# Two-part fused kernel: the last output products, the order of work in the first and last pair, and the change of parts are rearranged

## The reference, cut to what matters

```python
lat = layer_norm(_layernorm(x), g_lat, b_lat);  ctx = layer_norm(context, g_ctx, b_ctx)
q = lat @ Wq                       # 16 heads of 64
k, v = split(ctx @ Wkv);  k = apply_rope(k, cos, sin)
attn = softmax(clip(q @ k.T / 8, -11, 11))
x = x + (attn @ v) @ Wo + bo
h = _layernorm(x)
sel = sigmoid(h @ expert_sel.T)                 # (4, 512, 16)
scores = relu(einsum('bsd,edh->bseh', h, keys)) # 16 experts, 256 -> 128
out = x + einsum('bseh,ehv,bse->bsv', scores, values, sel)   # 128 -> 256
```

## Time and profile before

| | |
|---|---|
| runs | 1011.68, 1012.51, 1013.43 us |
| profiled execution, its own time | 1013.12 us |
| its span, first to last instruction | 1011.3 us |
| PE busy | 978.9 us, 97% |
| DVE busy | 809.5 us, 80% |
| ACT busy | 531.8 us, 53% |
| POOL busy | 146.1 us, 14% |
| mean granted clock of PE | 0.996 |
| attention, then experts | change of parts at 817 us |

### The profile page before, as it was taken

One profiled execution on the slowest core, in us unless ns is written; L12 is line 12 of the kernel. 1 busy time (PEld: TensorE's weight loads), 2 busy tenths in 40 slices (PEclk: granted clock), 3 DMA queues, 4 the chain that ended last, 5 costly groups with the idle time before them and its releaser, 6 DMA issues. The chain is left out here.

```text
span 1011.3 us, 16015 instructions
## 1 busy us (share of the span) xinstructions
PE 978.9 (97%) x5712; PEld 620.5 (61%) x5712; DVE 809.5 (80%) x1277; ACT 531.8 (53%) x765; POOL 146.1 (14%) x130
## 2 busy tenths in 40 slices
PE   4999999999999999999999999999999899999998
PEld 3744555555555555555555555555555368889898
DVE  7788999999999989898988887998889876545332
ACT  3666666566665666565656555555555532222221
POOL 3200000000000000000000000320000144444443
PEclk8999999999999999999999999999999999999999
DMA  7343323333232323333333223232222471342331
GB/s 217 111 132 95 111 85 110 103 102 88 77 90 74 89 74 97 89 99 79 97 83 90 64 85 84 84 84 84 85 63 65 131 266 54 126 126 84 115 113 44
DMA packets 68569, 99.84 MB, mean 99 GB/s; under 512 B 21840, under 2 KB 44624, under 8 KB 66448
## 3 DMA queue, kind: packets, MB, share of 16 engines
q1 hardware_dynamic: 68496, 98.89, 32.5%
HBM read 70.01 MB, written 10.75 MB: 80 GB/s over the span
## 5 line engine op out<-in xcount | busy, mean ns | idle before, releaser
L1099 ACT ACTIVATE wide_a<-score_ps 128x1024 f32<-128x1024 f32 x256 | 248.8, 1026 | 118.2 <-PE score_ps L859 118.0
L1401 DVE TENSOR_SCALAR wide_a<-wide_a 128x1024 f32<-128x1024 f32 x256 | 170.3, 691 | 48.1 <-ACT wide_a L1099 47.8
L1410 DVE TENSOR_TENSOR p_sum<-wide_a 128x1024 f32<-128x1024 f32 x128 | 158.5, 1238 | 2.4
L872 PE MATMUL o_ps<-wide_a,v_sb 128*64 128x512 f32 x512 | 124.0, 605 | 0.7 <-issue 0.6
L872 PE MATMUL o_ps<-wide_a,values_a 128*64 128x512 f32 x512 | 124.0, 605 | 0.2 <-issue 0.2
L859 PE MATMUL score_ps<-q_hi,k_hi 64*128 64x512 f32 x512 | 115.0, 445 | 3.3 <-ACT wide_a L1099 1.8
L859 PEld LDWEIGHTS score_ps<-q_hi,k_hi 64*128 64x128 f32 x512 | 47.9, 183 | 114.0 <-issue 79.5
L1917 DVE SCALAR_TENSOR_TENSOR act<-h_ps,wide_a 128x512 f32<-128x512 f32 x64 | 44.1, 690 | 89.2 <-PE h_ps L150 83.8
L1843 ACT CAST act_hi<-act 128x512 fp32r<-128x512 f32 x64 | 39.8, 622 | 138.1 <-DVE act L1917 138.1
L859 PE MATMUL score_ps<-q_hi,k_lo 64*128 64x512 f32 x512 | 101.1, 391 | 0.0
L859 PE MATMUL score_ps<-q_lo,k_hi 64*128 64x512 f32 x512 | 100.4, 388 | 0.0
(11 more groups left out here) (218 smaller groups left out, 1924.6 us busy)
## 6 DMA issues: line engine op xcount, KB each, us to landing
wide_a<-sel_dram SPq DMA_DIRECT2D x16, 1024.0 KB, 4.8
k_swap<-k SPq DMA_DIRECT2D x124, 128.0 KB, 2.3
w_hi<-packs_hi SPq DMA_DIRECT2D x26, 384.0 KB, 3.1
w_lo<-packs_lo SPq DMA_DIRECT2D x26, 384.0 KB, 3.7
den<-inv_dram SPq DMA_DIRECT2D x64, 128.0 KB, 2.9
ctx_raw<-ctx SPq DMA_DIRECT2D x24, 128.0 KB, 2.3
packs_hi<-w_hi SPq DMA_DIRECT2D x8, 384.0 KB, 2.9
packs_lo<-w_lo SPq DMA_DIRECT2D x8, 384.0 KB, 3.4
```

The source lines that it names most:

```text
L872: mm = pe.matmul(o_ps[DH * h:DH * h + DH, :], v_sb[n // 2 % 2][:, at:at + DH], probs[s % RING][:, h, :], start=(s == 0), stop=(s == STEPS ...
L1099: act.activation(probs[s % RING][:], score_ps[s % 2][:], ACT.Exp, scale=DH ** -0.5).then_inc(exp_done, 1)
L1401: dve.tensor_scalar(probs[s % RING][:], probs[s % RING][:], CLIP_HI, CLIP_LO, ALU.min, ALU.max).then_inc(clipped, 1)
L1410: dve.tensor_tensor(p_sum[m][:], first, second, ALU.add).then_inc(summed_up, 1)
```

## The change

In words, following the diff:

- `project_last_y` makes the last two output products (pairs 30 and 31) as one accumulation of six terms per half, at expert 14 of chunk 0. The product of pair 30, which was two products of three matmuls at the end of the attention part with two additions behind them, goes from there; so do two of the four last additions. The second buffers o_hi and o_lo are now shared by both parts.
- The first two expert products of chunk 0 are made at the end of the attention part, into job_ps[0] and job_ps[1]; `gate_h` reads them there. Turning y and x_n into these banks then waits for the gates. The fourth lot of keys has a semaphore of its own, waited on at expert 8.
- In pairs 24 to 27 `head_rows` (only the addition; the statistics are in `head_rows_stats`, at the old place) and `head_split_x` stand before the clips of step 3.
- In the first pair, `split_q(1)` stands after `sum_up` of step 1 and not ahead of `rope_times`, `split_v_weights(1)` after `stats`.
- In pairs 29 to 31, `split_o` stands before `add_y` and the sums of step 0. In the last pair the half product of pair 28 goes to job_ps[1] and that of pair 29 to job_ps[0]; the waits for y_added are loosened accordingly; `scale_o` stands after the second clip of step 3, the addition and `split_keys(3)` after the last sum; ACT rounds o and keys one step later; SP issues two loads of values after `turn_den` of pair 30 instead of before, and reorders the last loads.
- The last chunk's rows are stored in four transfers.

```diff
     product(pe, bank[:], [(hi, o_hi), (hi, o_lo), (lo, o_hi)]).then_inc(sh.y_projected, 1)
+def project_last_y(pe, sh, mt, bank, w_hi, w_lo):
+    wait(pe, sh.o_split, NPAIR)
+    terms = []
+    for n, at in ((NPAIR - 2, WO_AT), (NPAIR - 1, 0)):
+        hi, lo = w_hi[:, at + mt * P:at + mt * P + P], w_lo[:, at + mt * P:at + mt * P + P]
+        o_hi, o_lo = sh.o_hi[n % 2][:], sh.o_lo[n % 2][:]
+        terms += [(hi, o_hi), (hi, o_lo), (lo, o_hi)]
+    product(pe, bank[:], terms).then_inc(sh.y_projected, 1)
+def expert_terms(sh, e, x_hi, x_lo):
+    at = slice(e % 8 * HID, (e % 8 + 1) * HID)
+    terms = []
+    for k in range(KT):
+        hi, lo = sh.wide_hi[:, k, e // 8, at], sh.wide_lo[:, k, e // 8, at]
+        terms += [(hi, x_hi(k)), (hi, x_lo(k)), (lo, x_hi(k))]
+    return terms
...
                     turn_den(sp, sh, n - 1)
+                if n == NPAIR - 1:
+                    sp.wait_ge(pv_done, STEPS * (n - 1))
+                    for lot in (1, 2):
+                        sp.dma_start(sh.values_a[:, (lot - 1) * 4 * D:lot * 4 * D].rearrange("p (e d) -> p e d", d=D),
+                                     values[4 * lot:4 * lot + 4, :, :].rearrange("e h d -> h e d")
+                                     ).then_inc(sh.first_values[lot], DMA)
                 if n > 0:
...
                     load_keys(3)
-                    sp.wait_ge(pv_done, STEPS * n)
-                    for lot in (1, 2):
-                        sp.dma_start(sh.values_a[:, (lot - 1) * 4 * D:lot * 4 * D].rearrange("p (e d) -> p e d", d=D),
-                                     values[4 * lot:4 * lot + 4, :, :].rearrange("e h d -> h e d")
-                                     ).then_inc(sh.first_values[lot], DMA)
...
                 iteration(n)
-            sp.wait_ge(w_fetched, 2 * DMA * (NPAIR + 2 - PAIRS))
-            for dram, t in zip(packs, (sh.w_hi1, sh.w_lo1)):
-                sp.dma_start(raw(t)[:, 0:D], dram[(NPAIR - 1 + WO_LAG) % PAIRS, :, WO_AT:WC]).then_inc(sh.last_wo, DMA)
-            sp.wait_ge(k_split, NPAIR + 1)
-            sp.dma_start(k32[:].rearrange("p (e d) -> p e d", d=D),
-                         values[12:16, :, :].rearrange("e h d -> h e d")).then_inc(sh.first_values[3], DMA)
             sp.wait_ge(sh.gate_stored, DMA)
-            for q in range(2):
+            def first_gates(q):
                 sp.wait_ge(pv_done, STEPS * NPAIR - 2 + 2 * q)
...
                              ).then_inc(sh.first_gates[q], DMA)
+            first_gates(0)
+            sp.wait_ge(w_fetched, 2 * DMA * (NPAIR + 2 - PAIRS))
+            for dram, t in zip(packs, (sh.w_hi1, sh.w_lo1)):
+                sp.dma_start(raw(t)[:, 0:D], dram[(NPAIR - 1 + WO_LAG) % PAIRS, :, WO_AT:WC]).then_inc(sh.last_wo, DMA)
+            first_gates(1)
+            sp.wait_ge(k_split, NPAIR + 1)
+            sp.dma_start(k32[:].rearrange("p (e d) -> p e d", d=D),
+                         values[12:16, :, :].rearrange("e h d -> h e d")).then_inc(sh.first_values[3], DMA)
...
                 wait(pe, den_evac, n)
-                wait(pe, y_added, 2 * (n - 1))
+                wait(pe, y_added, 2 * (n - 1) - (1 if n >= NPAIR - 2 else 0))
                 if n == NPAIR - 1:
...
                 pe.wait_ge(den_evac, n)
-                pe.wait_ge(y_added, 2 * (n - 1))
+                pe.wait_ge(y_added, 2 * (n - 2) + 1)
                 ones_round([(0, p_sum[0]), (1, p_sum[1])], True, False)
...
                         pe.wait_ge(y_added, 2 * (n - 3) + 1)
-                        project_y(pe, sh, n - 3, 1, side_ps, w_hi[n % 2], w_lo[n % 2], (n - 1) % 2)
+                        project_y(pe, sh, n - 3, 1, job_ps[1] if n == NPAIR - 1 else side_ps, w_hi[n % 2], w_lo[n % 2],
+                                  (n - 1) % 2)
                     if m == 0 and p < NPAIR:
...
                     if m == 3 and n == NPAIR - 1:
-                        pe.wait_ge(y_added, 2 * (n - 2) + 1)
-                        project_y(pe, sh, n - 2, 1, side_ps, w_hi[p % 2], w_lo[p % 2], n % 2)
+                        pe.wait_ge(q_split, NPAIR)
+                        project_y(pe, sh, n - 2, 1, job_ps[0], w_hi[p % 2], w_lo[p % 2], n % 2)
                     if m > 0:
...
             pack_ready(NPAIR - 2 + WO_LAG)
-            for mt in range(2):
-                project_y(pe, sh, NPAIR - 2, mt, job_ps[mt], w_hi[1], w_lo[1], 0)
+            pe.wait_ge(sh.key_split, 3)
+            pe.wait_ge(head_split, 2)
+            pe.wait_ge(y_added, 2 * (NPAIR - 2))
+            for e in range(2):
+                product(pe, job_ps[e][:], expert_terms(sh, e, lambda k: xT_hi[:, 0, k, :], lambda k: xT_lo[:, 0, k, :])
+                        ).then_inc(sh.h_ready, 1)
...
                             round_keys((n - 24) // 2)
-                    if n == NPAIR - 1 and m in (1, 2):
-                        round_keys(m + 1)
+                    if n == NPAIR - 1 and m == 3:
+                        round_o(act, act.copy, sh, n - 1, 0)
+                    if n == NPAIR - 1 and m in (2, 3):
+                        round_keys(m)
...
                 iteration(n)
-            round_o(act, act.copy, sh, NPAIR - 2, 0)
             evac_o(NPAIR - 1)
...
                                   ALU.add).then_inc(head_added, 1)
+            def head_rows_stats(t):
...
                         normalize(t, ctx_n[:], x_n[:])
-                    if last and m == 3:
-                        add_y(dve, sh, n - 2, 1, side_ps, bo)
-                        split_keys(3)
+                    if m == 3 and n in (24, 25):
+                        head_rows(2 * (n - 24))
+                    if m == 3 and n in (26, 27):
+                        head_split_x(2 * (n - 26))
                     clip(n, 2 * m)
+                    if n == 0 and m == 0:
+                        rope_first_cos(1)
+                    if m == 1 and p < NPAIR:
+                        rope_times(p)
+                    clip(n, 2 * m + 1)
                     if last and m == 3:
...
                     if n == 0 and m == 0:
-                        rope_first_cos(1)
-                    if m == 1 and n == 0:
-                        split_q(p)
-                    if m == 1 and p < NPAIR:
-                        rope_times(p)
-                    clip(n, 2 * m + 1)
-                    if n == 0 and m == 0:
                         rope_first_sin(1)
+                    if m == 0 and n >= NPAIR - 3:
+                        split_o(dve, sh, n - 2, n % 2)
                     if m == 0 and n >= 3:
-                        add_y(dve, sh, n - 3, 1, side_ps, bo)
+                        add_y(dve, sh, n - 3, 1, job_ps[1] if last else side_ps, bo)
                     if m == 0 and n > 0 and n - 1 not in THREE_PARTS:
...
                         split_k_first(1)
-                        split_v_weights(1)
                     if m == 0:
...
                             stats(t)
-                        if n >= 2:
+                        if n == 0:
+                            split_v_weights(1)
+                        if 2 <= n < NPAIR - 3:
                             split_o(dve, sh, n - 2, n % 2)
...
                     if m == 1:
-                        if 0 < n < NPAIR - 1:
+                        if n < NPAIR - 1:
                             split_q(p)
...
                             invert_gate(dve, sh, 0, 1)
+                    if last and m == 3:
+                        add_y(dve, sh, n - 2, 1, job_ps[0], bo)
+                        split_o(dve, sh, n - 1, 0)
+                        split_keys(3)
                     if m == 3:
...
                         if n in (24, 25):
-                            head_rows(2 * (n - 24))
-                        if n in (26, 27):
-                            head_split_x(2 * (n - 26))
+                            head_rows_stats(2 * (n - 24))
...
                 iteration(n)
-            split_o(dve, sh, NPAIR - 2, 0)
-            for mt in range(2):
-                add_y(dve, sh, NPAIR - 2, mt, job_ps[mt], bo)
...
-            sp.wait_ge(sh.y_added, 2 * NPAIR)
+            sp.wait_ge(sh.y_added, 2 * NPAIR - 2)
             with sp.Fori(1, CHUNKS - 2) as c:
...
             chunk(CHUNKS - 1, last=True)
-            store(CHUNKS - 1)
-            sp.wait_ge(x_moved, DMA * (3 + 2 * CHUNKS))
+            for i in range(PER):
+                at = (CHUNKS - 1) * 512 + i * P
+                wait(sp, out_added, PER * (CHUNKS - 1) + i + 1)
+                sp.dma_start(out[at:at + P, :], x_out[i // 2][:, i % 2, :]).then_inc(x_moved, DMA)
+            sp.wait_ge(x_moved, DMA * (3 + 2 * CHUNKS + 2))
...
-            pe.wait_ge(sh.key_split, 4)
-            def expert_in(c, g, e):
-                wait(pe, gated, g - HRING + 1)
-                x_hi, x_lo = chunk_cols(xT_hi, c), chunk_cols(xT_lo, c)
-                at = slice(e % 8 * HID, (e % 8 + 1) * HID)
-                terms = []
-                for k in range(KT):
```

(27 more changed lines are left out.)

15 lines of the change are left out of this document (8 added, 7 removed).

## The result

The changed kernel took 1009.0 us (median of 6, 1005.63 to 1009.71), the kernel before beside it 1012.6: ratio 0.9955, 95% interval 0.9938 to 0.9971, so 4.6 us faster by that ratio, which is one of means; the medians differ by 3.6. The forecast was 1005.5 with a range of 1002.3 to 1009.3: the sign and the range hold, and two thirds of the forecast gain came by the ratio, half by the medians. The narrower range that the prediction gave the forecast itself, 1003.8 to 1007.0, does not hold: 1009 is its figure for rival D. The profiled execution took 1009.1 us with a span of 1007.3.

What follows compares the result with a forecast made beforehand. TensorE, busy 97% of the span, was taken as the bound. Gains of 2.6 (first pair), 3.2 (head rows), 1.1 (last pair, change of parts) and 0 (last stores) made 6.9 us, from median 1012.51 to 1005.5; range 1002.3 to 1009.3.

Steps and rivals of the forecast that it cites:

- rival D: Whole kernel: waits come back one queue later on DVE, half of each gain, 1009 us; chance 0.11.
- First pair: First pair's DVE reordering: the exponential wait goes, the "issue" wait shrinks by 0.5; gain 2.6 us, bounds 0 to 3.4.
- rival A: Second pair: early landings do not move, SP or DMA engines bound it, 1.8 us come back; 1008.1 us, chance 0.10.
- Head rows: Four places in pairs 24 to 27: PE waits of 3.9 us go, 0.7 handed back; gain 3.2, bounds 1.9 and 3.9.
- this hands back 0.4 and 0.3: First and third head places: PE's denominators wait for the later sum_quad, returning 0.4 and 0.3 us.
- Pairs 30 and 31: Early split_o costs 0.15 us before pair 30's denominators; in the last pair the 1.69 us yT wait goes.
- Last pair's queues: Inverse lands near 808.5, the last sum ends at 810.5, PE wants it at 811.6; 0.23 us wait goes.
- rival E: Last pair: the inverse's store behind value loads lands late, delaying scale_o(30), sum and PE; 1015.5 us, chance 0.03.
- Last pairs and change of parts: Last pair through expert 14: gap 0.3, x_n wait about 2.5, 1.4 us projection postponed; net gain 1.1, bounds -0.7 to 2.7.
- Rival B: After PE's idle stretch before turn_x: the clock falls to 1.2 GHz, losing 3.1 us; 1008.6 us, chance 0.11.
- Last stores: Kernel end: four stores of 128 KB for two of 256 give 0 us, between -0.4 and 0.4.
- a fall of PE's idle sum by less than 4 us: Whole kernel: a sign that the forecast is wrong and rival A or rival D holds; no separate chance.

Runs made afterwards that it cites:

- first_alone: The kernel before with only the first pair's reordering (split_q and split_v_weights behind ready work on DVE): 1011.96 us, ratio 0.9982.
- head_alone: The kernel before with only head_rows and head_split_x ahead of the clips of step 3 in pairs 24 to 27: 1009.96 us, ratio 0.9965.
- x_n_early: The changed kernel with DVE's residual and statistics ahead of its value splits, and POOL's power ahead of its activation split: 1008.82 us, ratio 0.9956.
- again: The changed kernel once more with no edit, timed and traced a second time: 1008.28 us, ratio 0.9949.
- after: The first profiled execution of the changed kernel, no further edit: 1009.1 us.
- change_alone: The changed kernel with the first pair's reordering and the head rows' reordering undone: 1013.24 us, ratio 0.9996.
- both: The changed kernel with the edits of keys_later and x_n_early together: 1006.39 us, ratio 0.9935.
- keys_later: The changed kernel with the second rounding of expert keys, and POOL's split behind it, moved from pair 26 to pair 27: 1007.76 us, ratio 0.9946.
- one_ahead: The changed kernel with keys_later's edit, reordered x_n chain, early split_o only in the last pair, one expert product behind the change of parts: 1004.63 us.

## Why the prediction was right, and where it was too high

- **First pair: right in mechanism, size within what one trace can tell.** rope_times stood at 43.56 (forecast 43.6), rope_add at 48.95 (48.5), the swap of pair 2 had landed by 68.11 (68.7), so rival A is out as to that landing. The wait for the exponential went entirely. The "issue" wait fell to 1.18 us, not 0.8: DVE's scaling ahead of split_weights(3) waits 1.74 us for an inverse of which the store took 3.0 us. The working read this wait as a matter of DVE's order and did not ask what the scaling waited for; where the store was punctual the whole wait went and the gain was 4.1 to 4.2 us, above the prediction's upper bound of 3.4. Forecast 2.6, first_alone 1.8 to 1.9. (The items of the working put rope_add at 48.3 and not 48.5; and rival A says that 1.8 us come back but charges 2.6.)
- **Head rows: right alone, 3.5 against 3.2; mis-sized in company.** The step "this hands back 0.4 and 0.3" failed for pair 26. The second figure was 0.88 and 0.92 us with a punctual store (head_alone, x_n_early), 1.78 to 2.07 with a late one, and in the profiled execution the whole wait returned as 2.75 + 1.2 us. The working took over the 2.1 us stretch of one sum, and no delay of the load ahead of it, though it named a late inverse for the last pair. In again, where the wait came back at the denominators, this is rival D's mechanism, in one place. That head_alone came out near the forecast is in part luck: 1.07 us were handed back and not 0.7, and the gain beyond the named waits made up for it. (The lower bound of 1.9, "the two large ones halved", should be 2.2, or 1.5 with what is handed back.)
- **Pairs 30 and 31: a wait of 0.5 to 0.8 us stood there in four traces with the early split, and a longer wait for k_lo in the other five, in place of 0.15 each time.** The slack of 0.5 us was read before PE moved ahead of a DVE that is busy without a gap there. The 1.69 us at yT went, as forecast.
- **Last pair's queues:** the load of the inverse came 0.19 us too late for DVE in the profiled execution, 1.29 us too late in again, where PE lost 0.43 us. The 0.23 us before the last denominators, which were to go, came back as 0.30 to 0.60 us in six of the eleven traces with this edit. The store behind the values took 2.5 to 3.6 us until the load in all eleven, against 1.42 before; rival E's chain exists at a tenth of its price.
- **Last pairs and change of parts, forecast a gain of 1.1 us: too high, and mostly of the wrong sign.** From pair 28 on the gain was 0.4, -0.1 and -0.4 us where the clock held (after, change_alone, x_n_early), -1.1 to -1.4 where it fell (again, both, keys_later). The gap was 0.33 (0.3) and the postponed projection 1.35 (1.4), both right; the wait at x_n was 2.0 (2.5), 0.5 us better than forecast. Mis-sized the other way were pair 30 (by 0.65) and the 0.35 us for the first split activation, which the sum left out.
- **Rival B, the clock (0.11), was half true:** with PE waiting at x_n 1.9 to 2.4 us the clock fell in three of six traces. Its price was 1.6 us in each of the three (in again PE went from 7.65 us ahead at 827 us to 6.09 at 830), not 3.1.
- **Last stores: 0.** They issue from 1003.7 to 1005.1 us and land 1.7 to 1.8 us later; from the last output product to the end of the span it is 3.6 us in both kernels.
- **Two of its own signs spoke against the forecast.** It named a fall of PE's idle sum by less than 4 us as one: span less busy time went from 32.4 to 28.8 us, 3.6 less, with the clock held at x_n; in again it went to 28.0, but there the granted clock dropped, its other sign. The range held because it was wide enough for rivals A, B and D, and because the first pair gave 0.3 to 0.5 us more than forecast.

The sum for the profiled execution is then 3.1 + 0.5 + 0.4 = 4.0 us, and for again 2.9 + 2.9 - 1.1 = 4.7 where the spans differ by 4.0 and 4.8; the sum of the forecast was 6.9. The largest part of the shortfall in the profiled execution is the head rows' 2.7 us.

## What to carry to other kernels

Price a move of work on a busy engine at each place where a second engine or a landing can hit the queue it now stands in, not at the place it leaves. Work put ahead of a change of parts helps only if the chain on the other side does not start from the change: here the wait went from 1.06 + 0.96 us to 0.33 + 2.0. Where a term is under 0.2% of the time, compare positions of the same instruction over several traces, with the unedited kernel's own scatter as the yardstick.

## What the runs showed of the hardware

- A 4 KB store to DRAM took 1.40 to 1.42 us until the next transfer for 29 of the 32 pairs before, but 2.8 to 3.6 us for pair 25 in 7 of the 14 traces and for pair 0 in 12 of them, with no other data transfer under way. The packets show why. The store is 128 packets of 32 bytes. In a punctual one all of them start 0.82 to 1.02 us after the issue. In each of these 19 late ones 120 do, and the last eight, a sixteenth of the store, start 1.6 to 2.7 us after it, within 0.1 us of the end of a 16 KB packet of the instruction queue, which took 0.9 to 1.4 us. In the nine punctual ones of these two pairs that packet starts only 1.18 us or more after the issue, behind the store's data. So a sixteenth of each late store waited until instructions had been loaded; this is read from 28 stores, no run tests it. GB/s of the DMA queues in 40 slices, in the changed kernel from 680.9 to 683.7 us (the 16 KB packet in the slice with 251, the last eight at the two slices with 2), and in one_ahead, punctual, from 679.5 to 680.9 us (the store first, then 468 for the packet):

```profile
GB/s 0 0 0 0 0 0 0 0 0 0 0 251 24 14 1 0 0 0 0 0 0 0 0 0 2 2 0 0 0 0 0 0 0 0 0 0 0 0 0 0
...
GB/s 0 0 0 0 0 0 0 0 0 0 0 0 0 0 0 0 0 0 0 0 0 0 0 16 35 25 23 16 4 0 0 0 0 468 0 0 0 0 0 0
```

- Why the packet meets the store in one execution and not in another is open. For pair 25 PE was 4.7 to 6.6 us ahead at pair 26 in the late ones, in the punctual ones 5.3 or at most 4.1.
- The granted clock fell behind PE waits of 1.92, 1.96, 1.99, 2.07, 2.27, 2.36 and 2.75 us, and held behind ones of 1.99, 2.00, 2.06, 2.17, 2.29 and 2.37 us. The length of a wait between 1.9 and 2.4 us doesn't tell which; the Trainium skill's page TensorE: Matmul & The Clock Gate, section "HAM oscillation — how this bites in real kernels", has the burst after an idle stretch start slow, which here holds for seven of the thirteen.
- POOL's 0.57 us power on 128 numbers took 1.49 us beside a DVE subtraction of two tiles in x_n_early, so the blocking goes both ways.
